# A product-key memory layer rebuilt from rank-one terms and small matrix products

## What is computed

```python
q = (xn @ w_q.T).reshape(b, n, 2, h, kd).transpose(2, 0, 1, 3, 4)
sim = jnp.einsum('pbnhd,hkpd->pbnhk', q, keys)      # h=8 heads, 32 keys on each of two sides
s, i = jax.lax.top_k(sim, k)                        # k=8
sx, sy = (s[0], s[1]); ix, iy = (i[0], i[1])
all_scores = (sx[..., :, None] + sy[..., None, :]).reshape(b, n, h, k * k)
all_idx = (ix[..., :, None] * nk + iy[..., None, :]).reshape(b, n, h, k * k)
scores, pk = jax.lax.top_k(all_scores, k)
idx = jnp.take_along_axis(all_idx, pk, axis=-1)
w_down = key_in[idx]; w_up = key_out[idx]           # tables of 1024 experts x 128
o = jnp.einsum('bnd,bnhkd->bnhk', inputs, w_down)
o = jax.nn.gelu(o, approximate=False) * jax.nn.softmax(scores, axis=-1)
return jnp.einsum('bnhk,bnhkd->bnd', o, w_up)
```

## Time and profile before

| | |
|---|---|
| median of 3 runs | 3413.17 us (3412.46 to 3413.53) |
| the profiled execution | 3410.9 us, with a span of 3409.2 us |
| busy over the span | PE 2896.7, DVE 2663.1, ACT 2300.4, POOL 1478.7 us |
| mean granted TensorE clock | 0.929 of full speed |
| memory stage, 662 to 1850 us | PE 897.1, DVE 992.8, ACT 860.0, POOL 1026.4 us of 1188 |

### The profile page before, as it was taken

One profiled execution on the slowest core, in us unless ns is written; L12 is line 12 of the kernel. 1 busy time (PEld: TensorE's weight loads), 2 busy tenths in 40 slices (PEclk: granted clock), 3 DMA queues, 4 the chain that ended last, 5 costly groups with the idle time before them and its releaser, 6 DMA issues.

```text
span 3409.2 us, 74113 instructions
## 1 busy us (share of the span) xinstructions
PE 2896.7 (85%) x23818; PEld 2181.0 (64%) x23818; DVE 2663.1 (78%) x6179; ACT 2300.4 (67%) x3434; POOL 1478.7 (43%) x837
## 2 busy tenths in 40 slices
PE   3999828677777777777777999989998999999999
PEld 2666515466666666666665666656667777777776
DVE  7999897888888888888887999976667666666665
ACT  2777635477777777777776666656666777777776
POOL 1333350188888888888886232224432000000000
PEclk9999958689899888899898999999996999999999
DMA  4000000000000000000001000000000000000000
GB/s 141 0 0 0 13 0 1 0 1 0 0 0 0 0 0 0 0 0 0 0 0 50 1 0 0 0 6 16 15 13 0 1 1 13 0 12 0 0 12 13
DMA packets 28639, 26.43 MB, mean 8 GB/s; under 512 B 4256, under 2 KB 23456, under 8 KB 28448
## 3 DMA queue, kind: packets, MB, share of 16 engines
q1 hardware_dynamic: 28576, 25.63, 2.5%
HBM read 21.43 MB, written 4.19 MB: 8 GB/s over the span
## 4 chain that ended last, share of the span: by engine, by line
PE 58%; POOL 19%; issue 16%; DVE 4%; ACT 1%; DVEq 1%; POOLq 0%; DMA 0%; ACTq 0%; SPq 0%
POOL work L485 17%; PE ps L839 7%; PE ps L1125 4%; PE ps L862 4%; PE ps L877 4%; PE ps L1094 3%; PE ps L850 3%; PE ps L1096 3%; PE ps L1095 3%; PE ps L1127 3%; PE ps L1126 3%; PE ps L890 2%; POOL work L474 2%; PE ps L1113 2%; PE ps L919 2%
## 5 line engine op out<-in xcount | busy, mean ns | idle before, releaser
L485 POOL TENSOR_TENSOR work<-work 128x1024 f32<-128x1024 f32 x512 | 963.3, 1916 | 150.2 <-DVE work L1541 150.1
L1014 PE MATMUL ps<-consts_sb,work 128*128 128x128 f32 x4096 | 557.1, 287 | 278.2 <-DVE work L1541 273.5
L1541 DVE SCALAR_TENSOR_TENSOR work<-work,ps 128x1024 f32<-128x1024 f32 x512 | 636.9, 1275 | 107.3 <-ACT ps L665 103.3
L1014 PEld LDWEIGHTS ps<-consts_sb,work 128*128 128x128 f32 x4096 | 473.2, 146 | 339.0 <-DVE work L1541 339.0
L439 POOL TENSOR_TENSOR work<-work,consts_sb 128x1024 f32<-128x1024 f32 x192 | 365.3, 1903 | 726.9 <-ACT work L549 552.9
L665 ACT ACTIVATE ps<-work 128x1024 f32<-128x1024 f32 x512 | 567.1, 1116 | 165.7 <-DVE work L1541 107.0
L1680 DVE TENSOR_TENSOR h_low<-consts_sb,h_up 128x1024 fp32r<-128x1024 f32 x128 | 158.4, 1237 | 190.6 <-ACT h_up L740 190.6
L839 PE MATMUL ps<-work 128*128 128x512 f32 x512 | 259.7, 609 | 3.2 <-issue 0.4
L1125 PE MATMUL ps<-h_low,d_up 128*128 128x512 f32 x512 | 214.4, 419 | 0.5 <-DVE h_low L1680 0.5
L1094 PE MATMUL ps<-a_low,w_up 128*128 128x512 f32 x512 | 203.4, 397 | 2.0 <-DVE a_low L1655 2.0
L1023 PEld LDWEIGHTS ps<-w,work 128*128 128x128 f32 x1024 | 150.9, 234 | 82.0 <-DVE work L1549 43.8
(11 more groups left out here) (254 smaller groups left out, 6279.3 us busy)
## 6 DMA issues: line engine op xcount, KB each, us to landing
ctxT_all<-in_ctxT SPq DMA_DIRECT2D x1, 4096.0 KB, 12.9
work<-in_ctx SPq DMA_DIRECT2D x64, 64.0 KB, 1.8
out<-x_all SPq DMA_DIRECT2D x4, 1024.0 KB, 5.1
big<-in_up SPq DMA_DIRECT2D x1, 2048.0 KB, 8.3
consts_sb<-in_consts SPq DMA_DIRECT2D x1, 936.0 KB
w<-in_key_inT SPq DMA_DIRECT2D x1, 512.0 KB, 3.8
w<-in_key_out SPq DMA_DIRECT2D x1, 512.0 KB, 5.1
rows_sb<-in_rows SPq DMA_DIRECT2D x1, 384.0 KB
```

The costliest lines, as they stand in the source:

```text
L485: pool.tensor_tensor(EE[:, h % HRING, :].rearrange("p (i j) -> p i j", i=NKEY), EX[:, T.u, a:a + NKEY].unsqueeze(2).to_broadcast([P, NKEY, ...
L1014: ins = pe.matmul(psG[:, c, :], WW[:, h % HRING, c * P:c * P + P], ident, is_transpose=True, start=h == 0 and c % 4 == 0, stop=h == PH - 1 ...
L1541: dve.scalar_tensor_tensor(out=WW[:, h % HRING, :], in0=EE[:, h % HRING, :], scalar=T8[:, T.u, h, TOPK - 1:TOPK], in1=psEP[h % 2], op0=ALU ...
```

## The change

Of two sorted lists, the pair (i, j) can be among the eight largest sums only if (i+1)(j+1) is at most 8, so i or j is 0 or 1. A head's chosen weights are therefore a sum of four rank-one terms: the best x key with all y keys, the second x key with all y keys, the remaining x keys with the best y key, and with the second y key. The change forms the 32 terms of 8 heads (4 x 8) as two lists of 32 keys for each token, and lets TensorE multiply them: a 32x32x32 product for each token.

- POOL: `outer` and `best_pairs` go. `candidates` forms 28 pairs a head; `terms` and `ranks` form the terms and the one-hot lists of best and second key, in nine instructions of 256 or 512 elements (three write `XY` with a step of 64 elements).
- ACT: `shares` scales 128 elements a head instead of 1024. `key_exps` is two instructions. Once per run ACT reorders the input table (`KI`).
- DVE: `chosen` works on 128 elements a head and writes with a step of 64 elements. `turn_sides` transposes the two lists in blocks of 32x32 (2 instructions of 1024 elements, written 32 elements apart); `turn_back` transposes the products' results (1 instruction of 1024 elements, read from PSUM).
- PE: the 64 transposes go. `spread_heads` does 128 products 32x32x32, on four groups of 32 partitions in turn, reading neighbouring elements and writing 16 elements apart into PSUM; `turn_weights` does 8 transposes.
- The lags grow from 2 to 3, the hidden values get a second buffer, `psM` moves from bank 6 to bank 4, which it shares with `psG`. The output table is loaded by four transfers in place of one, still in an earlier stage.

```diff
-        EE = carve(HRING * NEXP).rearrange("p (u n) -> p u n", u=HRING)
-        WW = carve(HRING * NEXP).rearrange("p (u n) -> p u n", u=HRING)
+        IN2 = carve(2 * NS).rearrange("p (s h k) -> p s h k", s=2, h=PH)
+        KI = carve(NEXP)
+        XY = carve(8 * NS).rearrange("p (k n h) -> p n h k", n=8, h=PH)
+        XT = carve(2 * NEXP).rearrange("p (u t k) -> p u k t", u=2, k=NKEY)
+        YT = carve(2 * NEXP).rearrange("p (u t k) -> p u k t", u=2, k=NKEY)
+        WT = carve(NEXP)
...
+        chosen_terms = XY[:, 2:6]
+        one_hot = [XY[:, n:8:6] for n in range(2)]
+        x_side, y_side = [XY[:, n:n + 4].rearrange("p n h k -> p k (n h)") for n in (0, 4)]
...
-        psEP = [ps[:, 2 * n:2 * n + 2, :].rearrange("p b n -> p (b n)") for n in range(2)]
+        psW = ps[:, 0:2, :].rearrange("p q (k t) -> p q k t", k=NKEY)
+        psSH = ps[:, 2:4, :].rearrange("p q (n h k) -> p (q n) h k", n=2, h=PH)
-        psM = bank(6, 0)
+        psM = bank(4, 0)
...
+            def candidates(T):
+                u = T.u
+                x, y = best_of(u)[:, 0], best_of(u)[:, 1]
                 pool.wait_ge(ex_ready, T.now())
-
-                best = EX[:, T.u, NS:].rearrange("p (n k) -> p n k", k=TOPK)
                 need(pool, t8_ready, T.before(1))
-                pool.tensor_tensor(CD.rearrange("p h (i j) -> p h i j", i=TOPK),
-                                   best[:, 0:PH].unsqueeze(3).to_broadcast([P, PH, TOPK, TOPK]),
-                                   best[:, PH:].unsqueeze(2).to_broadcast([P, PH, TOPK, TOPK]), ALU.mult).then_inc(cd_ready, 1)
-
-            def outer(first, last):
-
-                def seg(T):
-                    pool.wait_ge(ex_ready, T.now())
-                    for h in range(first, last):
-                        a, b = NKEY * h, NKEY * (PH + h)
-                        need(pool, ww_ready, T.step(PH, h + 1 - HRING))
-                        pool.tensor_tensor(EE[:, h % HRING, :].rearrange("p (i j) -> p i j", i=NKEY),
-                                           EX[:, T.u, a:a + NKEY].unsqueeze(2).to_broadcast([P, NKEY, NKEY]),
-                                           EX[:, T.u, b:b + NKEY].unsqueeze(1).to_broadcast([P, NKEY, NKEY]),
-                                           ALU.mult).then_inc(ee_ready, 1)
-                return seg
-            staggered(nc, pool, NT, [(1, outer(0, 6)), (0, best_pairs), (1, outer(6, PH))])
+                pool.tensor_tensor(CD[:, :, 0:TOP2 * TOPK].rearrange("p h (i j) -> p h i j", i=TOP2),
+                                   x[:, :, 0:TOP2].unsqueeze(3).to_broadcast([P, PH, TOP2, TOPK]),
+                                   y.unsqueeze(2).to_broadcast([P, PH, TOP2, TOPK]), ALU.mult)
+                pool.tensor_tensor(CD[:, :, TOP2 * TOPK:].rearrange("p h (i j) -> p h i j", i=DEEP),
+                                   x[:, :, TOP2:].unsqueeze(3).to_broadcast([P, PH, DEEP, TOP2]),
+                                   y[:, :, 0:TOP2].unsqueeze(2).to_broadcast([P, PH, DEEP, TOP2]), ALU.mult).then_inc(cand_ready, 1)
+
+            def terms(T):
+
+                u = T.u
+                x, y = keys_of(u)[:, 0], keys_of(u)[:, 1]
+                second = best_of(u)[:, :, :, 1:2].to_broadcast([P, 2, PH, NKEY])
+                rest, deep, wide = [terms_of(u)[:, n] for n in (REST, DEEP_X, WIDE_Y)]
+                need(pool, hot_ready, T.before(1))
+                pool.tensor_tensor(IN2, keys_of(u), second, ALU.subtract).then_inc(less_second, 1)
+                pool.tensor_tensor(wide, y, second[:, 0], ALU.mult)
+                pool.wait_ge(less_second, T.now())
+                pool.sem_inc(rank_seen, 1)
+                pool.tensor_scalar(IN2, IN2, 0.0, None, ALU.is_ge).then_inc(in2_ready, 1)
+                pool.wait_ge(in2_ready, T.now())
+                pool.sem_inc(rank_seen, 1)
+                pool.tensor_scalar(rest, IN2[:, 0], -1.0, 1.0, ALU.mult, ALU.add).then_inc(far_ready, 1)
+                pool.wait_ge(far_ready, T.now())
+                pool.tensor_tensor(rest, rest, x, ALU.mult).then_inc(rest_ready, 1)
+                pool.wait_ge(rest_ready, T.now())
+                pool.tensor_tensor(deep, rest, second[:, 1], ALU.mult).then_inc(terms_ready, 1)
+
+            def ranks(T):
+
+                u = T.u
+                need(pool, sides_ready, T.before(1))
+                pool.tensor_tensor(one_hot[0], keys_of(u), best_of(u)[:, :, :, 0:1].to_broadcast([P, 2, PH, NKEY]), ALU.subtract)\
+                    .then_inc(less_top, 1)
+                pool.wait_ge(less_top, T.now())
+                pool.sem_inc(rank_seen, 1)
+                pool.tensor_scalar(one_hot[0], one_hot[0], 0.0, None, ALU.is_ge).then_inc(top_ready, 1)
+                pool.wait_ge(top_ready, T.now())
+                pool.tensor_tensor(one_hot[1], IN2, one_hot[0], ALU.subtract).then_inc(hot_ready, 1)
+            staggered(nc, pool, NT, [(0, candidates), (0, terms), (0, ranks)])
...
+                first, y = EX[:, u, 0:BEST + NS], keys_of(u)[:, 1]
+                act.activation(first, first, ACT.Exp)
+                act.activation(y, y, ACT.Exp).then_inc(ex_ready, 1)
+            def shares(T):
+                u = T.u
+                act.wait_ge(rz_ready, T.now())
+                act.wait_ge(terms_ready, T.now())
+                need(act, xy_ready, T.before(1))
+                for h in range(PH):
+                    ins = act.activation(psSH[:, :, h, :], terms_of(u)[:, :, h, :], ACT.Copy, scale=RZ[:, u, h:h + 1])
+                ins.then_inc(share_ready, 1)
...
+            staggered(nc, act, NT, [(0, normed), (1, shares), (0, key_exps), (1, hidden)])
...
+            def spread_heads(T):
+
+                pe.wait_ge(sides_ready, T.now())
+                need(pe, back_ready, T.before(1))
+                pe.sem_inc(pe_seen, 1)
+                for n in range(BLOCK):
+                    for g in range(P // BLOCK):
+                        rows = slice(BLOCK * g, BLOCK * g + BLOCK)
+                        ins = pe.matmul(psW[rows, n // 16, :, n % 16], XT[rows, T.u, :, n], YT[rows, T.u, :, n], start=True, stop=True)
+                ins.then_inc(spread_done, 1)
+
+            def turn_weights(T):
+                pe.wait_ge(back_ready, T.now())
+                need(pe, hg_ready, T.before(1))
+                need(pe, y_used_m, T.before(1))
+                for c in range(CHUNKS):
+                    ins = pe.transpose(psG[:, c, :], WT[:, c * P:c * P + P], ident)
+                ins.then_inc(back_turned, 1)
...
-            staggered(nc, pe, NT, [(0, key_scores), (2, mixed), (1, gates(0, 2)), (1, hidden), (1, gates(2, PH))])
+            staggered(nc, pe, NT, [(0, key_scores), (2, spread_heads), (1, hidden), (3, mixed), (2, turn_weights)])
...
+            def chosen(T):
+
+                u = T.u
+                dve.wait_ge(share_ready, T.now())
+                for h in range(PH):
+                    ins = dve.scalar_tensor_tensor(out=chosen_terms[:, :, h, :], in0=terms_of(u)[:, :, h, :],
+                                                   scalar=T8[:, u, h, TOPK - 1:TOPK], in1=psSH[:, :, h, :],
+                                                   op0=ALU.is_ge, op1=ALU.mult)
+                ins.then_inc(xy_ready, 1)
+
+            def turn_sides(T):
+
+                dve.wait_ge(xy_ready, T.now())
+                dve.wait_ge(hot_ready, T.now())
+                need(dve, spread_done, T.before(2))
+                dve.transpose(XT[:, T.u], x_side)
+                dve.transpose(YT[:, T.u], y_side).then_inc(sides_ready, 1)
+
+            def turn_back(T):
+
+                dve.wait_ge(spread_done, T.now())
+                need(dve, back_turned, T.before(1))
+                dve.transpose(WT, psW.rearrange("p q k t -> p k q t")).then_inc(back_ready, 1)
...
-            staggered(nc, dve, NT, [(1, chosen(0, 1)), (2, gated), (0, top_keys), (0, less_best), (1, chosen(1, 2)), (2, add_memory),
-                                    (1, chosen(2, 6)), (0, top_pairs), (0, pair_sums), (1, chosen(6, 7)), (0, pair_shares),
-                                    (1, chosen(7, PH))])
+            staggered(nc, dve, NT, [(0, top_keys), (0, less_best), (1, chosen), (2, turn_back), (0, top_pairs), (3, add_memory),
+                                    (1, turn_sides), (0, pair_sums), (2, gated), (0, pair_shares)])
```

More of the change, by code:

```diff
@@ L20 @@
 NKEY = 32
-HRING = 4
+BLOCK = 32
 PH = 8
@@ L400, in _ @@
             sp.dma_start(kin, key_inT).then_inc(tables, 16)
-            sp.dma_start(kout, key_out.rearrange("(c p) d -> p c d", p=P)).then_inc(tables, 16)
+            for j in range(P // NKEY):
+                sp.dma_start(kout[NKEY * j:NKEY * j + NKEY], key_out.rearrange("(a c j) d -> j a c d", a=NKEY, c=CHUNKS)[j])\
+                    .then_inc(tables, 16)
             sp.wait_ge(phase, PHASE["attn1"])
@@ L654, in key_exps @@
             def key_exps(T):
+                u = T.u
                 act.wait_ge(d_ready, T.now())
[L656 to L666 removed]
```

(5 more changed lines are left out.)

91 lines of the change are left out of this document (39 added, 52 removed).

## The result

The changed kernel takes 3092.87 us (median of 4 runs, 3091.18 to 3094.15), the kernel before 3413.35 beside it: a ratio of 0.9059, 95% interval 0.9044 to 0.9075. It is 9.4% faster. The forecast was 3207 us with a range of 3093 to 3383, so the time lies 0.13 us under the range: the direction was right, the size was not.

A forecast was written before the change was run, and what follows sets the result against it. POOL's outer products set the old 18.31 us period; afterwards PE would bound at 15.1 us a tile. Stage 63p + 32.3 = 983.6 us against 1190.3, so 3207 us in all, range 3093 to 3383.

The forecast's parts named there:

- PE's term for the products: PE, spread_heads: 256 matrix records a tile at 29 ns each plus 0.2, 7.6 us.
- the lower end, 3.8 us: PE, products of a tile: half the 7.6 us, if time went with the columns.
- PE's sum: PE, per tile: 5.3 staying + 7.6 products + 1.1 transposes + 0.5 + 0.3 waits and handoffs = 14.8 us, rounded up to 15.1.
- DVE's 14.0: DVE, per tile: 5.6 + 2.95 chosen + 3.9 turns + 1.2 turn_back + 0.5 waits - 0.2 = 14.0 us.
- my own formula: Whole kernel: time is 2255.2 + 63p us, p being the period of a tile; before is met at p = 18.38.
- a granted clock near 1.00: PE in the changed stage: over 95% busy, so granted the full clock; gain under 0.5 us left as cover.
- The fixed part, 32.3: Stage time outside 63 periods: 27 + 15 - 11 + 1.3 = 32.3 us, for draining, one period, first iterations and reordering.
- Rival 3: PE and DVE: products at 3.8 us and no charge for steps, p = 12.8, 3062 us; chance 0.10.
- Rival 2: DVE becomes the bound through its stepped writes, p = 16.5, 3295 us; chance 0.22.
- Rival 1: PE's queue: long bursts of small products bound by record issue, 67 ns each, p = 20.0, 3515 us; chance 0.18.
- Rival 4: Loop DVE, POOL, DVE: engines wait for one another, the change moves nothing, p near 18.3; chance 0.05.
- 0.7 ns an element: DVE's stepped writes in chosen and the turns: 0.7 ns an element charged, from a stepped read; a turn 1.95 us.

The follow-up runs named there:

- same_quarter: Changed kernel with the same 128 products issued as 32 in a row on one quarter of the array, not quarters in turn: 3704.86 us, ratio 1.0856.
- products_twice: Changed kernel with each of a tile's 128 products done twice into the same place: 3863.11 us, ratio 1.1321.
- filler: Changed kernel with two more 128x512 products a tile on PE, results overwritten, put ahead of the wait for the turned sides: 3067.08 us, ratio 0.8985.

## Why the prediction was wrong, step by step

The step that failed is PE's term for the products, "256 x 0.029 + 0.2 = 7.6 us". It measured 2.34 us at full clock and 2.9 in the mean. The 29 ns came from pairs of 64-wide products that use two halves of the array in turn and from products that use all its rows; four quarters in turn go at 9.0 ns, as `same_quarter` shows. The prediction says that the new products work on quarters, and yet it took the price of halves; one quarter by itself takes 31 ns at full clock, so 29 ns is about the price without any overlap. Even the lower end, 3.8 us, was too dear. The other steps:

- PE's sum is 2.34 + 2.05 + 1.95 + 1.06 + 1.02 = 8.4 us at full clock, not 14.8. It doesn't set the period. With DVE's 14.0 in its place my own formula gives 2255.2 + 63 x 14.0 = 3137 us.
- DVE's 14.0 was too high as well. The groups of new work sum to 2.25 + 3.83 + 1.23 = 7.3 us a tile, where I had 2.95 + 3.9 + 1.2 = 8.05: the turns and `turn_back` were right within 0.1, but `chosen`, which writes 64 elements apart, shows no price for that in a row (2.25 us for 8, or 0.28 each, what L1427 costs; one by itself lasts 422 ns against 335). The other part is that I added durations, and neighbours on one engine overlap: L1611 starts at 1212.45, lasts 1.96 and L1612 starts at 1214.25, 0.16 us before its end. Over a tile DVE's groups sum to 12.9 us and it is busy 11.87.
- The clock. I forecast a granted clock near 1.00 because PE would be over 95% busy. It is busy 605 of 867 us, and the clock is 0.86. That a busy PE is granted the full clock doesn't hold either: see `same_quarter`, 88% busy at 0.67. The long fourth tiles cost 0.47 us each tile in the mean, and `filler` got nearly all of it back.
- The period is thus 12.3 (DVE) + 0.5 (clock) = 12.8, and with the stage's first tiles 12.99: 63 x (14.0 - 12.99) = 64 us under the 3137. 
- The fixed part, 32.3, measured 51: 49 from the last scores to the end, where I had 42; the first scores 2.1 us later (663.9 for 661.8), where I had 1.3 for the reordering; and the 11 us that I took off for the first two tiles, which the measured mean already holds. 2255.2 + 63 x 12.99 + 18.9 = 3092.5, the measured time; it must come out, since 12.99 and 51 are themselves measured. The first tiles do skip the products, the first taking 6.1 us, but later ones of the unrolled beginning take up to 18.9, and there PE stands for its instructions as in `products_twice`, 16.3 us in all. No term of mine had that.

Rival 3 (both cheaper than charged, p = 12.8, 0.10) comes nearest, and in part by luck. That the products are cheap is right in kind. But its 12.8 was POOL's upper end, and POOL has 10.6 us; its DVE of 11.9 left out the price of the steps, which the turns do pay (3.83 us, not 2.5), and meets the measured 11.87 only because overlapping instructions save about as much. Of the 31 us that its 3062 lacks, 19 are the fixed part and 12 the first tiles. Rival 2 is right that DVE becomes the bound, at 12.3 us and not at 16.5, and wrong on the cause: the steps cost no more than I charged. Rival 1's 67 ns a record is not there: the long burst goes at 9 ns. On one quarter a record takes 48 ns, and the kernel is slower than before already there, below that rival's limit of 62 ns, because PE's other work pays for the low clock too (`hidden` 3.66 us and `mixed` 2.69 a tile, for 2.05 and 1.95 at full clock). Rival 4 is out: p fell by 5.3 us.

On order: `turn_back` follows the end of the products with 9.7 us of waiting in all, as worked out. What I missed is that `hidden` waits for `less_best` (51.6 us), and that `add_memory` stands behind `hidden` on PE; I had called both ahead of `turn_weights` harmless cover and didn't ask who waits for `mixed`. POOL's 10.6 us and ACT's 7.2 a tile were not above what I gave them, and both are hidden.

Of a step in a turn's output I had 0.7 ns an element, and the turns cost 1.90 and 1.84 ns for each of their 1024, against 1.20 and 1.17 with neighbours: 0.7. That estimate was good for the turns and wrong for `chosen`.

## What to carry to other kernels

Small products are priced by the part of the array that they follow each other on: issue them with the partition group as the inner loop, and look in the trace for rows of the same pattern before taking a price from others. When an engine gets lighter, ask again which one leads, and for that one behind which entry of another engine's list the work stands that it waits for; an edit of order that wins alone can lose beside another. A step belongs on the engine with slack: here the products read apart for 1.5 us that PE had to spare, and DVE's tile became 1.1 us shorter (12.3 to 11.2).

## What the runs showed of the hardware that I had not expected

- Idle gaps of PE of some 2 us a tile go with a granted clock of 0.50 in stretches; work that nobody needs (2 products a tile) raised it from 0.90 to 1.00 in the middle of the stage and made the kernel 26 us faster. Small products on one quarter were granted 0.67 with PE 88% busy.
- A loop whose body grows by 256 products on PE (128 for each of its two tiles, 512 records) had its instructions fetched anew on each turn: 373 packets instead of 49, and stops of 1.5 to 1.8 us after 128 records in a row.
- Products that read 32 elements apart took 3.85 us for 256 records at full clock and 3.86 at 0.56; with neighbours it was 2.34 at full clock and 3.64 at 0.50.
- POOL's comparison of 512 elements took 1.49 us between neighbours (L523), 2.06 writing apart and reading neighbours, and 2.38 reading and writing apart.
- A short DVE instruction with two operands in SBUF took 0.80 us instead of 0.29 where it began 0.4 us after a POOL comparison, and 1.28 where it began 0.5 us after a POOL subtraction.
- PSUM writes of a 32x32 product 16 elements apart cost nothing that these runs can tell.
